# Counting each gather's own end instead of a small write behind it, in a three-layer graph network kernel

## The reference

```python
def _rgcn_layer(x, W, SW, b, src, dst, rel):
    xt = jnp.einsum('nd,rde->rne', x, W)
    msg = xt[rel, src]
    agg = jax.ops.segment_sum(msg, dst, num_segments=x.shape[0])
    return jax.nn.relu(agg + x @ SW + b)
x = _layernorm(x + rgcn(rgcn(x)))            # w1, sl1, b1, then w2, sl2, b2
feat = jax.nn.relu(x @ W1 + b1)
h = feat * d_invsqrt                         # by the node's degree
agg = jax.ops.segment_sum(h[src], dst, num_segments=N)
out = _layernorm(x + (feat - agg * d_invsqrt) @ W2 + b2)
```

## Time and profile before

| | us |
|---|---|
| the runs, median of 3 | 7370.4 |
| the runs, lowest and highest | 7354.83, 7371.55 |
| span of the profiled execution | 7320.2 |
| GpSimd busy in it | 5851.5 (80%) |
| TensorE matmuls busy | 3691.2 (50%) |
| TensorE weight loads busy | 2669.6 (36%) |
| VectorE busy | 1720.1 (23%) |
| ScalarE busy | 409.6 (6%) |

### The profile page before, as it was taken

How to read it: one execution, slowest core, us unless ns; L and a number is a source line. 1 busy time by engine, 2 the same in 40 slices (tenths; PEclk the granted TensorE clock), 3 DMA queues, 4 the chain that set the end, 5 groups by cost and what they waited for, 6 DMA issues and landing times.

```text
span 7320.2 us, 56431 instructions
## 1 busy us (share of the span) xinstructions
PE 3691.2 (50%) x13687; PEld 2669.6 (36%) x13841; DVE 1720.1 (23%) x2844; ACT 409.6 (6%) x915; POOL 5851.5 (80%) x9940
## 2 busy tenths in 40 slices
PE   4555555555555556556565555554424333433343
PEld 3333333333333333334343333433323333333333
DVE  4333333333333212222222222221101111111111
ACT  1000000000000100000000000010000000000000
POOL 7888888888888588888888888867888888888887
PEclk7666667676666777767677776675555555555555
DMA  2111111111111112211222221211111111111111
GB/s 66 49 51 52 50 50 50 51 52 50 50 52 51 40 49 57 56 56 55 56 58 56 56 57 56 56 54 42 51 51 52 51 51 51 51 51 53 51 51 48
DMA packets 197585, 382.88 MB, mean 52 GB/s; under 512 B 84322, under 2 KB 93326, under 8 KB 197542
## 3 DMA queue, kind: packets, MB, share of 16 engines
q0 software_dynamic: 159456, 326.88, 17.0%
q1 hardware_dynamic: 36416, 54.67, 2.1%
q10 hardware_dynamic: 1670, 0.85, 0.0%
HBM read 356.43 MB, written 25.65 MB: 52 GB/s over the span
## 4 chain that ended last, share of the span: by engine, by line
POOL 48%; issue 20%; another core or an unknown queue 20%; PE 7%; DVE 3%; DVEq 1%; POOLq 0%; ACT 0%; DMA 0%; ACTq 0%; SPq 0%
POOL rows L794 39%; POOL pause L798 9%; PE bank L980 3%; PE bank L950 3%; DVE r_S L1042 1%; DVE r_hot L1037 1%; PE bank L1205 1%; ACT r_agg L904 0%; PE bank L1440 0%; PE bank L964 0%; DVE acc L1081 0%; DMA acc<-in_dst_dram 0%; DVEq L1071 0%; POOLq L109 0%
## 5 line engine op out<-in xcount | busy, mean ns | idle before, releaser
L794 POOL DMA_INDIRECT rows<-in_x_dram,idx x1661 | 1588.6, 956 | 466.9 <-issue 396.7
L794 POOL DMA_INDIRECT rows<-x_d,idx x1647 | 1574.2, 956 | 453.5 <-issue 397.8
L794 POOL DMA_INDIRECT rows<-h_d,idx x1640 | 1566.9, 955 | 441.4 <-issue 396.3
L980 PE MATMUL bank<-r_S,rows 128*128 128x128 f32 x6644 | 1408.2, 380 | 705.1 <-issue 486.8
L1205 PE MATMUL bank<-r_S,rows 128*128 128x64 f32 x3322 | 821.9, 388 | 1332.3 <-issue 1079.4
L980 PEld LDWEIGHTS bank<-r_S,rows 128*128 128x128 f32 x6644 | 1299.5, 285 | 501.4 <-issue 482.1
L1205 PEld LDWEIGHTS bank<-r_S,rows 128*128 128x128 f32 x3322 | 775.1, 315 | 1378.0 <-issue 1272.4
L798 POOL MEMSET pause<- 128x128 f32 x4948 | 1096.3, 222 | 4.3 <-issue 0.2
L1042 DVE TENSOR_TENSOR r_S<-bank,key 128x1792 f32<-128x1792 f32 x238 | 480.4, 2019 | 1225.9 <-remote 1080.3
L964 PEld LDWEIGHTS bank<-zeros_bf 128*128 128x128 bf16 x476 | 54.1, 114 | 1463.0 <-issue 1056.8
L964 PE MATMUL bank<-zeros_bf 128*128 128x512 bf16 x323 | 174.9, 542 | 722.4 <-issue 505.8
(11 more groups left out here) (152 smaller groups left out, 1471.1 us busy)
## 6 DMA issues: line engine op xcount, KB each, us to landing
rows<-in_x_dram,idx POOLq DMA_INDIRECT x1661, 3.3
rows<-x_d,idx POOLq DMA_INDIRECT x1647, 3.4
rows<-h_d,idx POOLq DMA_INDIRECT x1640, 3.4
d_xr<-in_x_dram SPq DMA_DIRECT2D x54, 218.0 KB
x_d<-d_yr SPq DMA_DIRECT2D x27, 218.0 KB
d_x1r<-x_d SPq DMA_DIRECT2D x27, 218.0 KB
h_d<-d_hr SPq DMA_DIRECT2D x27, 218.0 KB
part_d<-d_pr SPq DMA_DIRECT2D x27, 218.0 KB
```

The costliest lines, as they stand in the source:

```text
L794: pool.indirect_dma_start(out=self.c.rows[:, self.place(s), :], out_offset=None, in_=self.table[:, :], in_offset=bass.IndirectOffsetOnAxis ...
L980: mm = pe.matmul(agg_ps[j][:, bass.ds(offs[j * KG + k], TK)], c.rows[:, g.place(h * KG + k), :], S[:, pb, j * KG + k, :], start=False, sto ...
```

## The change

```diff
+AHEAD = 3
-        c.pause = sb("pause", [P, PT, P])
-        self.rest = PAIR if then is None else 1
-        self.paused = sem("paused")
+        self.written = sem("written")
...
                 pool.wait_ge(self.idx_ready, (q * (IT + 1) + i) * PR + p + 1)
                 pool.wait_ge(self.summed, self.pairs_summed(q, i, p))
                 gate(pool, self.c.passed)
                 for h in range(p * PAIR, (p + 1) * PAIR):
-                    if (h + 1) * KG <= skip:
-                        if h % rest == rest - 1:
-                            pool.sem_inc(self.paused, 1)
-                        continue
-                    if h % rest == 0:
-                        pool.wait_ge(self.paused, q * (NG // rest) + i * (RING // rest) + h // rest + 1)
-                        gate(pool, self.c.passed)
                     for k in range(part.of(h)):
                         s, slot = h * KG + k, h if k < halves(part, h) else RING + h % PAIR
                         if s < skip:
                             continue
+                        pool.wait_ge(self.written, q * TILES + i * UN + s + 1)
+                        gate(pool, self.c.passed)
                         pool.indirect_dma_start(
                             out=self.c.rows[:, self.place(s), :], out_offset=None, in_=self.table[:, :],
-                            in_offset=bass.IndirectOffsetOnAxis(ap=self.c.idx[:, at + s:at + s + 1], axis=0)
+                            in_offset=bass.IndirectOffsetOnAxis(ap=self.c.idx[:, at + s:at + s + 1], axis=0),
+                            engine_sem=self.written
                         ).then_inc(self.landed[slot], 16)
-                        ins = pool.memset(self.c.pause[:, s % PT, :], 0.0)
-                    if h % rest == rest - 1:
-                        ins.then_inc(self.paused, 1)
...
-        pool.sem_inc(self.paused, 1)
+        pool.sem_inc(self.written, AHEAD + EARLY[self.turns])
...
-        pool.wait_ge(self.paused, rounds * (NG // rest) + 1)
+        pool.wait_ge(self.written, rounds * TILES + AHEAD)
```

More of the change, by code:

```diff
@@ L769, in run @@
     def run(self, pool, ready, stored):
-        rest = self.rest
         def iteration(q, i, part, set_of, skip=0):
@@ L776, in iteration @@
                 if (p + 1) * PT <= skip:
-                    pool.sem_inc(self.paused, PAIR // rest)
                     continue
```

## The result

The changed kernel took 7556.7 us (7554.4 to 7567.5, four runs) against 7366.3 (7354.8 to 7371.6, four runs): a ratio of 1.026, interval 1.025 to 1.028. It is slower; the forecast was 6632, with a range of 6480 to 7010.

A forecast was written before the change was run, and what follows sets the result against it. GpSimd's line was taken as the kernel's length. Saving 873 us, less 25 at section starts and 110 for TensorE, left 738: span 7320.2 to 6582, plus 50.2 gave 6632, range 6480 to 7010.

The forecast's parts named there:

- Memsets, gap, period: On GpSimd, 4,948 memsets of 222 ns go; gathers of 0.95 us with 0.30 idle then start every 1.25 us.
- The wait and its gate are hidden: Before each gather on GpSimd: handing out costs 0.81 us, hidden under 2.80 us of gathers in hand.
- the third rival: At each gather's gate: the wait empties GpSimd's queue, period 1.76 us, +1519 us, 8890 in all; chance 0.05.
- The gather's own count costs nothing and comes at its end: At each gather's semaphore: counting adds nothing; upper bound, the count comes only with the landing, 3.4 us behind the start.
- The first rival: At each gather's count: it comes with the landing, period 1.40 us, 138 us less, 7230 in all; chance 0.06.
- The second gap of 1.07 is covered: Before a gather about every 101 us on GpSimd: late handing out, hidden by two gathers in hand, 63 us saved.
- The sum, 873 us: GpSimd's line: 4,948 x 1.2515 = 6192 plus 127 of other waits, 6319 against 7192, if nobody else is late.
- What is late next (b): At the full ring: TensorE's slow stretches make GpSimd wait 55, 15 and 40 us in the three sections, 110 together.
- (a): At each section's start: the ring is full before TensorE begins, so about 25 us of the saving is waited out.
- The 50.2 us: Between the profiled span and the median of the runs: added to the forecast span of 6582 to give 6632.
- The second, TensorE becomes the bound: TensorE's slow first-section iterations stay at 80 us or more: 350 to 400 us less, about 7000; chance 0.23.
- The fourth: At the full ring: all saved time is waited out, no difference, 7350 to 7390; chance 0.02.

The follow-up runs named there:

- e6: The changed kernel with AHEAD = 1 instead of 3, each gather waiting for the one before, on chip 7: 8913 us, ratio 1.248.
- e4: The kernel before with two of the eight matmuls of each mix, on chip 8: 7125 us, ratio 0.998.
- e5: The changed kernel, unedited, against the kernel before on chip 7: 6305 us, ratio 0.882.
- e13: The changed kernel with only the first gather of each group of seven, without the waits before gathers and engine_sem, on chip 5: 3255 us.
- e16: The changed kernel with two of the eight matmuls of each mix, on chip 5, a single run: 7431 us.
- e9: The changed kernel with each relation's matmul of a mix made six times over, on chip 9: 11283 us.
- e10: The kernel before with each relation's matmul of a mix made six times over, on chip 9: 9768 us.
- e14: The changed kernel without engine_sem, with a counting memset behind each gather (one every 1.34 us), on chip 5: 7484 us, ratio 1.036.
- e7: The changed kernel with the wait and gate only before the first gather of each group of 7, on chip 7: 6288 us, ratio 0.880.
- e18: The changed kernel without engine_sem, with a counting memset of 448 columns behind each gather, on chip 11: 8026 us, ratio 1.089.
- e15: The changed kernel with AHEAD = 1, a gather every 1.75 us, on chip 5, a single run: 8905 us.

## Why the prediction was wrong, by its own steps

**Memsets, gap, period: right.** 0.94 to 0.95 busy and 0.30 idle, 1.25, on every chip.

**The wait and its gate are hidden: right.** One wait for seven gathers makes 6288 of 6305. The price without cover, 0.81, and the period of the third rival, 1.76, were measured in e6 as 0.81 and 1.75.

**The gather's own count costs nothing and comes at its end: right.** e6's period of 1.75 us is shorter than any landing in its trace (2.4 us at the least, median 2.6). By the rule of the Trainium skill that the prediction quoted (Perfetto Trace Analysis, DMA Instruction — SWDGE (GPSIMD)), the profiled end is the last descriptor. The trace agrees in that the end is not the landing; that the count goes with this end is the run's, with the next start 0.81 us behind it. The first rival is out.

**The second gap of 1.07 is covered: right.** On chip 7 the waits of GpSimd that nobody ends are 48.9 us in all, and the gap of 1.07, which the kernel before has every 101 us in the first profile and, on chip 8, in e4, is not in e5's timeline.

**The sum, 873 us: right in size, on a chip without the disturbance.** There e5's span of 6294.4 is 4948 x 1.2515 = 6192 and 102 of other time, where the forecast had 127 + 25 + 110 and what lies outside the gathers. Against the kernel before on that chip the time fell by 840 us, 11.8%, more than the forecast's 738 and 10.0%, since neither the start nor TensorE cost anything. The periods alone, 7002 - 6192, are 810 of it. As a ratio, 0.882, this lies just inside the forecast's range (6480 / 7370 = 0.879), as a time, 6305, below it, for the kernel before is 225 us faster there than the forecast's base.

**"What is late next (b)" failed.** This is the step that put the forecast on the wrong side. Its sentence is "a TensorE with a full ring in front of it is the fast one", its term 110 us. On the first chip the third section of the changed kernel has TensorE standing 1250.7 us before its own instructions, and it is slow right behind a full ring too. By sections, first to last gather: 2500, 2464 and 2389 us instead of 2170, 2090 and 2175, 918 in all; 53 more lie in the joins and the end. That makes the 971 us between the forecast span, 6582, and 7552.8. The start is part of it: (a) had 25 us, and the 57th gather alone waits 53.94.

The 50.2 us that the forecast put on top of its span were no time outside the span. In the later runs, which have both numbers, the time is about 2 us above the span of the same execution (7554.74 and 7552.8). So the first profile had caught an execution faster than the runs beside it.

I had the sign before me and read it as the clock. The earlier trace rows fit that: 0.84 in the fast stretch, 0.69 in the slow. But the two stretches of the third section in the earlier trace rows have one and the same clock in the kernel before:

```profile
5115.00:5124.00 9.00, 8.00 (x37) 7.80 (x37) 3.06 (x7) 0.41 (x2) 7.04 (x12) 0.50 0.14 36
5137.00:5177.00 40.00, 9.69 (x38) 9.63 (x38) 5.47 (x18) 0.70 (x3) 33.15 (x57) 0.50 0.21 59
```

37 matmuls in 9 us, and 38 in 40 us, both at 0.50, the lower level of 1.2 GHz. GpSimd's share is much the same as well, 7.04 of 9 us and 33.15 of 40, so nothing in these rows tells the stretches apart but the pace. And this row of the page before, which I left out of the argument, holds the answer's size:

```profile
L1205 PE MATMUL bank<-r_S,rows 128*128 128x64 f32 x3322 | 821.9, 388 | 1332.3 <-issue 1079.4
```

1079 us of "issue" on an engine that should be waiting for rows. On an undisturbed chip the kernel before with the short mix has none there.

**The rivals.** The second, TensorE becomes the bound, is nearest in looks (the full ring, iterations of over 80 us) and wrong in cause: e13 and e16 show that its work isn't. Its 7000 rested on the gain in the second section, which did not come either. The fourth would need the same pace in all sections, which was there, but it gave 7350 to 7390 and no loss. The slower side had 0.07, and all but 0.02 of that for a mechanism of GpSimd's own. No case had the gathers slow down their readers, and none had the answer depend on the chip.

**Why slower and not equal.** In the third section both kernels run at the ceiling. The rest of the loss lies in the first two, (1567.6 + 935.5) / 1661 = 1.51 and (1553.4 + 920.2) / 1647 = 1.50 us a gather, in the starts, where the changed kernel writes the whole ring at 1.25 us and then waits, and in the joins, 166 instead of 124 us. That a stream which runs over the ceiling and is stopped is worse than an even one is what this suggests, and e9 against e10 points the same way. It is not shown: an evenly spaced gather at 1.45 us was not run, and e14, even at 1.34 with 7484, is no better than the changed kernel.

**What stays open.** What it is of a gather that disturbs (the writing of its descriptors, the transfers themselves, or their counting), why weight loads of TensorE, and many gathers, then start multiples of 0.70 us apart, and why two of six chips are free of it, or were when they were measured. Whether it would be there without the profiler is open as well, since each run was recorded; the times of runs and profiles agree. Gathers of fewer rows and other places for the table in memory were not tried. No version with all its gathers beats the kernel before on a disturbed chip. On the others e7 beats both, by a margin over the changed kernel that its interval doesn't settle.

## What to carry to other kernels

When the bound engine is made faster, ask what its output does to the others at the new rate, and look for the sign in the trace of before: idle time ended by "issue" on an engine whose data is there. Compare two stretches of the same instructions at the same granted clock before putting a slow one down to the clock. A comparison on one chip holds for that chip at that time: the unedited kernel belongs beside every later run, or experiments explain a difference that no edit made.

## What the runs showed of the hardware

- The same program takes different times on different chips, each measured at one time: 7138 and 7145 us on two, 7220, 7225 and 7229 on three, 7369 on one. For the changed kernel the gap is larger, 6305 to 7557.
- On four of six chips long rows of gathers of 128 rows (`DMA_INDIRECT`, 0.95 us each) handed out every 1.25 or 1.34 us go with 909 to 1423 us of "issue" idle time before TensorE's matmuls in the third section, and the first comparison shows the same, with weight loads that start 1.41 or 2.10 us apart in such spells, where e5 on chip 7 takes 3.06 us for a block of 14. At 1.60 us (e18) and 1.75 us (e15), or with 8 gathers in an iteration of 41 us (e13), it is gone.
- A semaphore given to a gather as `engine_sem` is counted by the gather's profiled end, before its rows have landed, and a gather that waits for it starts 0.81 us behind that end (e6).
- A GpSimd memset of 128x448 took 488 ns, one of 128x128 222.
